# A vision layer on one core: one signal of TensorE for both halves of a product, and a new order of the work

## The chip, the cores and the metric

The kernel runs on one core of a Trainium2 chip. The metric is the device time of one execution in microseconds, lower is better. TensorE multiplies, VectorE and ScalarE work on its results, GpSimd issues gathers and computes small powers, SyncE loads and stores. Each engine executes its own list of instructions in order, and semaphores tie the lists together.

## The reference, cut to what matters

64 images of 3 x 224 x 224 are cut into 196 patches of 768 numbers each. Everything is float32.

```
h = patches @ W.T + b                                   # 768 -> 256
x = layernorm(h); xn = x / rms(x) * g
u, v, base = silu(xn @ uv_w.T)                          # 512 + 512 + 128
q, k = rope(base * gamma + beta)
kern = relu((q @ k.T + w_rel) / sqrt(128)) ** 2         # 196 x 196 per image
h = h + x * res_scale + (u * (kern @ v)) @ o_w.T
x = layernorm(h); logits = x @ W_in.T + b_in            # 8 trees of 255 nodes
walk each tree from its root by the signs of the logits (8 nodes visited)
h = h + (silu(logits) at the visited nodes, 0 elsewhere) @ W_out.T
```

## The kernel before, in words

Two images make a unit of T = 392 columns; there are 32 units. The hidden state is kept transposed, as two halves (m = 0, 1) of 128 features by 392 columns. A float32 product is made of three matmuls (`product`, lines 1144 to 1146): each operand is split into a high and a low part, ScalarE makes the high part (`high`, line 530), VectorE the low part (`low`, line 837).

The work is a software pipeline. In one pass of the loop, unit n is embedded and normalized (front), unit i goes through attention and starts its trees, and unit p = i - 1 finishes its trees. The passes at both ends, where p, i or n do not exist, are written out. The order of the calls in the four `body` functions (GpSimd, ScalarE, VectorE, TensorE) is written out, and it is the order in which each engine executes. Units are shifted between the lists: a pass of ScalarE and VectorE begins at about the middle of TensorE's.

What the change and the steps of the prediction touch:

- PSUM is full. `out_acc` sums the trees' outputs (2 banks), `hid_ps` holds two trees' logits and visits, or the embedding (4 banks), and `front` (2 banks) is used in turn by turned h, turned xn, the normalized rows turned back, base, v, u, scores, the mix, the o projection and the trees' input.
- `turn_h` turns h so that rows are tokens, for the statistics (`norm_stats`, `norm_moments` on VectorE, the power -1/2 in `norm_roots` on GpSimd, `norm_apply` and `make_xn` on ScalarE). `turn_xn` turns the result back (line 1186, eight transposes, four for each half); `xn_high` and `xn_low` split it. `turn_normed` overwrites each half of `front` with the layer norm turned back, and so waits for `xn_low` of that half; `residual` (line 901) adds it to h, and `make_base` waits for the first `residual`.
- Each of the 8 trees goes through `tree_logits`, `decisions` (line 982, the signs), `tree_visits` (line 1339, one bf16 matmul that counts how far each node is on the path), `silu_tree` (line 685), `mask` (lines 993 and 998), `hid_high`, `hid_low` and `tree_out`. Two buffers alternate, so `hid_high(i, t)` waits until `tree_out` of two trees before is whole.
- In the first four trees only the upper half of the nodes is computed; the leaf's rows are gathered: `find_leaf` (line 1368) and `leaf_number` (line 703) make the row numbers, `fetch_rows` on GpSimd (line 476) issues four indirect DMAs a tree, `leaf_dots` (line 1017), `leaf_silu` and `scale_rows` (line 720) weigh the rows, and `add_rows` (line 1380) adds them to `out_acc`.
- `project_o` makes the o projection, `update_h` (line 964) adds it to h. `turn_ffn_x` turns the trees' input.
- In the first units GpSimd also splits the late weights (`late_splits`, lines 442 and 445), and `build_rows` on ScalarE fills the table of the gathers.

TensorE signals at the end of each of these pieces; in `turn_h`, `turn_back`, `project_o` and `tree_out` at the end of each half m.

Of the kernel before, what the change touches and what calls it, by code (L numbers as in the profile page):

```python
# [44 lines left out]
DC = D // P  # L45
# [70 lines left out]
def vit_tower(nc, x, cols, tok_w, uv_w, o_w, in_w, out_w, rel, rope, anc, ident_in, out):  # L116
    ctx = ExitStack()
    with ctx:
# [317 lines left out]
        def _(pool):  # L436
# [51 lines left out]
            def body(p, i, n, nx):  # L488
                late_splits(i, n, 0)
                late_splits(i, n, 1)  # L490
                fetch_rows(i, 0, 0)
                fetch_rows(i, 0, 2)
                fetch_rows(i, 0, 1)
                fetch_rows(i, 0, 3)
                late_splits(i, n, 2)
                fetch_rows(i, 1, 0, n)
                fetch_rows(i, 1, 2)
                fetch_rows(i, 1, 1)
                fetch_rows(i, 1, 3)
                late_splits(i, n, 3)  # L500
                fetch_rows(i, 2, 0)
                fetch_rows(i, 2, 1)
                fetch_rows(i, 2, 2)
                fetch_rows(i, 2, 3)
                late_splits(i, n, 4)
# [22 lines left out]
        def _(act):  # L528
# [203 lines left out]
            def body(p, i, n, nx):  # L732
# [5 lines left out]
                if first(n):  # L738
                    build_rows()
                silu_tree(p, 7, 0)  # L740
                scale_rows(p, 3)
                silu_tree(i, 0, 0)
                hid_high(p, 7)
                norm_apply(n, 0, 0)
# [5 lines left out]
                make_xn(n, 1)  # L750
                silu_tree(i, 2, 0)
                norm_apply(n, 0, 2)
                norm_apply(n, 0, 3)
                make_xn(n, 2)
                make_xn(n, 3)
                hid_high(i, 1)
                x_high(nx, 0)
                xn_high(n, 0)
                silu_tree(i, 3, 0)
                leaf_number(i, 1)  # L760
                xn_high(n, 1)
                leaf_number(i, 2)
                x_high(nx, 1)
                hid_high(i, 2)
                silu_base(n)
                silu_v(n, 0)
                scale_base(n, 1)
                leaf_silu(i, 0)
                scale_rows(i, 0)
                silu_v(n, 1)  # L770
                v_high(n, 0)
                v_high(n, 1)
                scale_base(n, 0)
                silu_tree(i, 4, 1)
                hid_high(i, 3)
                silu_v(n, 2)
                v_high(n, 2)
                silu_v(n, 3)
                qk_high(n, 0)
                qk_high(n, 1)  # L780
                silu_u(n, 0)
                leaf_number(i, 3)
                v_high(n, 3)
                silu_tree(i, 4, 0)
                silu_tree(i, 5, 1)
                silu_u(n, 1)
# [5 lines left out]
                x_high(nx, 2)  # L792
                hid_high(i, 4)
                silu_u(n, 3)
                silu_tree(i, 5, 0)
                mix_high(n, 0)
                mix_high(n, 1)
                hid_high(i, 5)
                mix_high(n, 2)
                silu_tree(i, 6, 1)  # L800
                mix_high(n, 3)
                silu_tree(i, 6, 0)
                keep_h(i)
                leaf_silu(i, 2)
                x_high(nx, 3)
                scale_rows(i, 2)
                x_high(nx, 4)
                hid_high(i, 6)
                leaf_silu(i, 3)
                x_high(nx, 5)  # L810
# [3 lines left out]
                norm_apply(n, 1, 3)  # L814

# [19 lines left out]
        def _(dve):  # L835
# [216 lines left out]
            def body(p, i, n, nx):  # L1052
                norm_stats(n, 0, 0)
                norm_stats(n, 0, 1)
                norm_moments(n, 0)
                decisions(i, 0)
                decisions(i, 1)
                mask(i, 0)
                hid_low(p, 7)
                decisions(i, 2)  # L1060
                mask(i, 1)
                if first(n):
                    build_toward()
                hid_low(i, 0)
                decisions(i, 3)
                mask(i, 2)
                final(p)
                hid_low(i, 1)
                xn_low(n, 0)
# [4 lines left out]
                leaf_dots(i, 0)  # L1074
                rotate_qk(n, 1)
                decisions(i, 4)
                mask(i, 3)
                v_low(n, 0)
                decisions(i, 5)
                v_low(n, 1)  # L1080
                rotate_qk(n, 0)
# [3 lines left out]
                hid_low(i, 3)  # L1085
                leaf_dots(i, 1)
                mask(i, 4)
                v_low(n, 3)
                add_rel_bias(n, 0)
                add_rel_bias(n, 1)  # L1090
# [4 lines left out]
                x_low(nx, 0)  # L1095
                hid_low(i, 4)
                mask(i, 5)
                gate(n, 0)
                mix_low(n, 0)
                gate(n, 1)  # L1100
                decisions(i, 6)
# [4 lines left out]
                hid_low(i, 5)  # L1106
                mix_low(n, 3)
                x_low(nx, 1)
                leaf_dots(i, 2)
                x_low(nx, 2)  # L1110
                mask(i, 6)
                update_h(n, 0)
                update_h(n, 1)
                norm_stats(n, 1, 0)
                norm_stats(n, 1, 1)
                norm_moments(n, 1)
                x_low(nx, 3)
                leaf_dots(i, 3)
                x_low(nx, 4)
                decisions(i, 7)  # L1120
# [20 lines left out]
        def _(pe):  # L1141
# [25 lines left out]
            def turn_h(n, which, m):  # L1167
# [13 lines left out]
                last.then_inc(h_turned, 1)  # L1181

            def turn_back(src, m, done):
# [4 lines left out]
                last.then_inc(done, 1)  # L1188
# [96 lines left out]
            def project_o(n, m, es):  # L1285
# [12 lines left out]
                if es[-1] == EC - 1:  # L1298
# [43 lines left out]
            def tree_out(i, t, m):  # L1342
# [14 lines left out]
                last.then_inc(tree_added, 1)  # L1357
# [38 lines left out]
            def body(p, i, n, nx):  # L1396
                make_u(i, 0)
                tree_visits(p, 4)
                make_u(i, 1)
                tree_logits(p, 5, 1)  # L1400
                tree_out(p, 3, 0)
                tree_logits(p, 6, 0)
                scores(i, 0)
                scores(i, 1)
                tree_logits(p, 6, 1)
                add_rows(p, 1)
                tree_visits(p, 5)
                make_u(i, 2)
                make_u(i, 3)
                tree_out(p, 3, 1)  # L1410
                mix(i, 0)
                mix(i, 1)
                tree_out(p, 4, 0)
                mix(i, 2)
                mix(i, 3)
                tree_out(p, 4, 1)
                tree_visits(p, 6)
                project_o(i, 0, range(0, 3))
                project_o(i, 0, range(3, EC))
                project_o(i, 1, range(0, EC))  # L1420
                tree_logits(p, 7, 0)
                embed(n, 0)
                turn_h(i, 1, 0)
                turn_h(i, 1, 1)
                embed(n, 1)
                tree_logits(p, 7, 1)
                embed(n, 2)
                tree_out(p, 5, 0)
                embed(n, 3)
                embed(n, 4)  # L1430
                embed(n, 5)
                turn_ffn_x(i, 0)
                turn_ffn_x(i, 1)
                tree_out(p, 5, 1)
                tree_visits(p, 7)
                add_rows(p, 2)
                turn_h(n, 0, 0)
                turn_h(n, 0, 1)
                tree_out(p, 6, 0)
                tree_logits(i, 0, 0)  # L1440
                tree_logits(i, 1, 0)
                if first(n):
                    turn_rows()
                tree_visits(i, 0)
                tree_out(p, 6, 1)
                tree_logits(i, 2, 0)
                add_rows(p, 3)
                find_leaf(i, 0)
                tree_visits(i, 1)
                tree_out(p, 7, 0)  # L1450
                tree_visits(i, 2)
                tree_logits(i, 3, 0)
                find_leaf(i, 1)
                tree_out(p, 7, 1)
                tree_logits(i, 4, 0)
# [7 lines left out]
                tree_out(i, 1, 1)  # L1463
                tree_visits(i, 3)
                turn_normed(n, 1)
# [3 lines left out]
                tree_out(i, 2, 0)  # L1469
                make_v(n, 1)  # L1470
                make_v(n, 2)
                tree_logits(i, 5, 0)
                make_v(n, 3)
                tree_out(i, 2, 1)
                add_rows(i, 0)
                find_leaf(i, 3)
# [92 lines left out]
```

## Time and profile before

| | us |
|---|---|
| median of 3 runs | 2083.43 |
| lowest, highest | 2078.61, 2083.67 |
| profiled execution | 2077.75 |
| its span | 2075.9 |
| TensorE busy | 2034.1 (98%) |
| VectorE busy | 1626.5 (78%) |
| ScalarE busy | 1403.7 (68%) |
| GpSimd busy | 728.1 (35%) |

The span is the time from the first to the last instruction of the profiled execution. Busy time is a union of the rows of an engine, and matmuls overlap in their rows, since each is shown with the time that it takes through the array. In the rows PE is TensorE, DVE VectorE, ACT ScalarE, POOL GpSimd and SP SyncE.

### The profile page before, as it was taken

What the parts mean: (1) busy time and instruction counts of PE and PEld (TensorE: products, weight loads), DVE (VectorE), ACT (ScalarE), POOL (GpSimd) and SP (SyncE); (2) the same over time, 40 slices, a digit from 0 to 9 for tenths busy, and PEclk for the clock granted to TensorE, in tenths of its full rate; (3) what the DMA queues carried; (4) which work ended last, traced back from release to release, by engine and by line L of the source; (5) the groups of instructions that cost most, each with busy time, mean ns of one, the idle gap of its engine ahead of it and who ended that gap; (6) DMA issues with size and microseconds to landing.
All of it is one profiled execution on the core that took longest, in us unless ns stands there. A gap on an engine that the chain in (4) does not pass through costs nothing. (4 is left out here: it accounts for less than half of the span.)

```text
span 2075.9 us, 42491 instructions
## 1 busy us (share of the span) xinstructions
PE 2034.1 (98%) x13256; PEld 1918.2 (92%) x13256; DVE 1626.5 (78%) x4210; ACT 1403.7 (68%) x3085; POOL 728.1 (35%) x905
## 2 busy tenths in 40 slices
PE   6899999999999999999999999999999999999997
PEld 5799999999999999999999999999999999999997
DVE  5678878787877888777878787878778887778785
ACT  5556677667676667776666776676766667666665
POOL 3553343233332333333323432333323333333333
PEclk8999999999999999999999999999999999999999
DMA  5222232223222223222222322232222232222222
GB/s 159 82 80 80 82 85 67 69 70 92 81 75 68 77 70 86 80 74 70 73 81 81 85 66 70 70 93 80 74 70 77 70 85 81 74 68 72 73 71 78
DMA packets 81999, 163.13 MB, mean 79 GB/s; under 512 B 17102, under 2 KB 48048, under 8 KB 81968
## 3 DMA queue, kind: packets, MB, share of 16 engines
q0 software_dynamic: 40960, 103.02, 18.7%
q1 hardware_dynamic: 41008, 59.71, 9.7%
q8 instruction: 17, 0.28, 0.1%
q14 instruction: 14, 0.11, 0.0%
HBM read 148.76 MB, written 13.90 MB: 78 GB/s over the span
## 5 line engine op out<-in xcount | busy, mean ns | idle before, releaser
L476 POOL DMA_INDIRECT leaf_rows<-leaf_table,leaf_at x512 | 528.8, 1033 | 186.2 <-issue 186.2
L453 POOL TENSOR_TENSOR inv_root<-to_root,minus_half 98x8 f32<-98x8 f32 x64 | 94.8, 1481 | 748.7 <-DVE to_root L877 428.2
L1144 PE MATMUL out_acc<-hid_hi,outw_lo 128*128 128x392 f32 x768 | 285.4, 372 | 0.3 <-issue 0.2
L1144 PE MATMUL hid_ps<-ffn_x,in_lo 128*128 128x392 f32 x768 | 268.1, 349 | 7.9 <-POOL in_lo L445 6.9
L1145 PE MATMUL hid_ps<-ffn_x,in_hi 128*128 128x392 f32 x768 | 262.3, 342 | 0.0
L1146 PE MATMUL out_acc<-hid_hi,outw_hi 128*128 128x392 f32 x768 | 262.3, 341 | 0.0
L1145 PE MATMUL out_acc<-hid_lo,outw_hi 128*128 128x392 f32 x768 | 261.8, 341 | 0.0
L1146 PE MATMUL hid_ps<-ffn_x,in_hi 128*128 128x392 f32 x768 | 260.8, 340 | 0.0
L685 ACT ACTIVATE hid<-hid_ps,col 128x392 f32<-128x392 f32 x256 | 150.8, 589 | 124.0 <-DVE decide L982 89.0
L837 DVE TENSOR_TENSOR hid_lo<-hid,hid_hi 128x392 fp32r<-128x392 f32 (+1 forms) x256 | 197.4, 771 | 39.5 <-ACT hid_hi L530 38.8
L720 ACT ACTIVATE leaf_rows<-leaf_rows,leaf_act 98x256 f32<-98x256 f32 x512 | 218.7, 505 | 2.2
L998 DVE SCALAR_TENSOR_TENSOR hid<-hid_ps,hid 128x392 f32<-128x392 f32 x384 | 202.6, 554 | 3.4 <-remote 2.4
L1017 DVE CUSTOM_DVE_ANT_0 leaf_rows<-leaf_rows,leaf_x 98x257 f32<-98x257 f32 x512 | 188.2, 422 | 2.9 <-DMA leaf_rows<-leaf_table,leaf_at 2.9
L530 ACT ACTIVATE hid_hi<-hid 128x392 fp32r<-128x392 f32 (+1 forms) x256 | 176.0, 687 | 5.9 <-DVE hid L998 3.0
L530 ACT ACTIVATE x_hi<-x_raw 128x392 fp32r<-128x392 f32 x192 | 100.7, 525 | 111.8 <-PE hid_ps L1146 110.5
L982 DVE TENSOR_SCALAR decide<-hid_ps,col 128x392 bf16<-128x392 f32 x256 | 158.7, 620 | 21.1 <-PE hid_ps L1146 16.6
L475 POOL TENSOR_TENSOR held<-minus_half 98x1 f32<-98x1 f32 x128 | 33.0, 258 | 386.8 <-ACT v_full L616 185.5
L1144 PEld LDWEIGHTS hid_ps<-ffn_x,in_lo 128*128 128x128 f32 x768 | 144.9, 189 | 14.1 <-POOL in_lo L445 7.8
L1144 PEld LDWEIGHTS out_acc<-hid_hi,outw_lo 128*128 128x128 f32 x768 | 146.0, 190 | 2.9 <-issue 0.5
L1145 PEld LDWEIGHTS hid_ps<-ffn_x,in_hi 128*128 128x128 f32 x768 | 144.8, 188 | 2.8
L1145 PEld LDWEIGHTS out_acc<-hid_lo,outw_hi 128*128 128x128 f32 x768 | 145.7, 190 | 1.5
L530 ACT ACTIVATE xn<-u 128x392 fp32r<-128x392 f32 x128 | 68.2, 533 | 115.1 <-DVE u L949 111.2
(140 smaller groups left out, 5840.6 us busy)
## 6 DMA issues: line engine op xcount, KB each, us to landing
x_raw<-x SPq DMA_DIRECT2D x192, 196.0 KB, 2.4
out<-out_stage SPq DMA_DIRECT2D x32, 392.0 KB
leaf_rows<-leaf_table,leaf_at POOLq DMA_INDIRECT x512
leaf_table<-leaf_rows SPq DMA_DIRECT2D x4, 256.5 KB, 5.3
out_stage<-in_w SPq DMA_DIRECT2D x4, 256.0 KB
tok_major<-tok_w SPq DMA_DIRECT2D x3, 256.0 KB, 4.8
late_raw<-out_w SPq DMA_DIRECT2D x6, 128.0 KB
u<-uv_w SPq DMA_DIRECT2D x1, 576.0 KB, 3.8
```

The source lines that it names most:

```text
L453: pool.tensor_tensor(inv_root[:, 0:size], to_root[:, 0:size], minus_half[:, 0:size], ALU.pow).then_inc(roots_ok, 1)
L476: pool.indirect_dma_start(row_slot(s, g), None, table, bass.IndirectOffsetOnAxis(ap=leaf_at[:, s, g:g + 1], axis=0), element_offset=s * P ...
L530: act.activation(out, src, ACT.Copy).then_inc(done, 1)
L685: act.activation(hid_t[:, t % 2, b], hid_ps[:, t % 2, b, 0:T], ACT.Silu, bias=bias).then_inc(activated, 1)
L720: act.activation(w, w, ACT.Copy, scale=leaf_act[:, s, g:g + 1]).then_inc(rows_scaled, 1)
L837: dve.tensor_tensor(out, src, hi.bitcast(F32), ALU.subtract).then_inc(done, 1)
L982: dve.tensor_scalar(decide[:, t % 2], hid_ps[:, t % 2, 0, 0:T], c(COL_B_IN + 2 * t), 0.0, ALU.add, ALU.is_gt).then_inc(decided, 1)
L998: dve.scalar_tensor_tensor(hid_t[:, t % 2, b], hid_ps[:, t % 2, 1, 0:T], VISITED[b], hid_t[:, t % 2, b], ALU.is_ge, ALU.mult).then_inc(mas ...
L1017: dve.tensor_tensor_reduce(w, w, normed2[:, g], 1.0, 0.0, ALU.mult, ALU.add, leaf_logit[:, s, g:g + 1]).then_inc(dotted, 1)
L1144: pe.matmul(out, w[1], x_parts[0], start=start, stop=False)
L1145: pe.matmul(out, w[0], x_parts[1], start=False, stop=False)
L1146: return pe.matmul(out, w[0], x_parts[0], start=False, stop=stop)
```

## The change

TensorE gives 64 signals a unit in place of 77. `tree_out`, `turn_h`, `project_o`, `turn_xn` and `turn_ffn_x` signal once, behind the second half, and whoever waited for a half now waits for both. `turn_normed` keeps its two signals. And the order of the calls in all four `body` functions is another.

```diff
@@ scalar
-                act.wait_ge(xn_turned, 2 * n + m + 1)
+                act.wait_ge(xn_turned, n + 1)
...
-                act.wait_ge(ffn_x_turned, 2 * n + m + 1)
+                act.wait_ge(ffn_x_turned, n + 1)
...
-                    act.wait_ge(tree_added, 2 * (TREES * i + t - 1))
+                    act.wait_ge(tree_added, TREES * i + t - 1)
@@ vector
-                dve.wait_ge(h_turned, 2 * (2 * n + which) + m + 1)
+                dve.wait_ge(h_turned, 2 * n + which + 1)
...
-                dve.wait_ge(projected, 2 * n + m + 1)
+                dve.wait_ge(projected, n + 1)
...
-                dve.wait_ge(tree_added, 2 * TREES * (i + 1))
+                dve.wait_ge(tree_added, TREES * (i + 1))
@@ tensor, turn_h
-                last.then_inc(h_turned, 1)
+                if m == DC - 1:
+                    last.then_inc(h_turned, 1)
@@ turn_back
-                last.then_inc(done, 1)
+                if m == DC - 1 or done is normed_turned:
+                    last.then_inc(done, 1)
@@ project_o
-                if es[-1] == EC - 1:
+                if m == DC - 1 and es[-1] == EC - 1:
                     last.then_inc(projected, 1)
@@ tree_out
-                last.then_inc(tree_added, 1)
+                if m == DC - 1:
+                    last.then_inc(tree_added, 1)
```

The new order of TensorE, whole (a pass; products of unit p, then i, then n as named):

```
tree_visits(p, 4); tree_logits(p, 5, 1); make_u(i, 0..1); tree_out(p, 3, 0); scores(i, 0..1)
tree_logits(p, 6, 0); make_u(i, 2..3); tree_visits(p, 5); tree_logits(p, 6, 1); mix(i, 0..3)
add_rows(p, 1); tree_out(p, 3, 1); tree_visits(p, 6); project_o(i, 0, 0..2); tree_logits(p, 7, 0)
project_o(i, 0, 3); project_o(i, 1, all); embed(n, 0); tree_out(p, 4, 0); turn_h(i, 1, 0..1)
embed(n, 1); tree_out(p, 4, 1); embed(n, 2..4); tree_logits(p, 7, 1); embed(n, 5)
turn_ffn_x(i, 0..1); tree_out(p, 5, 0..1); tree_visits(p, 7); turn_h(n, 0, 0..1)
tree_logits(i, 0, 0); tree_logits(i, 1, 0); tree_out(p, 6, 0); tree_visits(i, 0)
tree_logits(i, 2, 0); add_rows(p, 2); tree_out(p, 6, 1); find_leaf(i, 0); tree_visits(i, 1)
add_rows(p, 3); tree_out(p, 7, 0); tree_visits(i, 2); tree_out(p, 7, 1); find_leaf(i, 1)
tree_logits(i, 3, 0); tree_logits(i, 4, 0); turn_xn(n, 0..1); find_leaf(i, 2)
tree_out(i, 0, 0..1); tree_out(i, 1, 0); turn_normed(n, 0); tree_out(i, 1, 1); turn_normed(n, 1)
tree_visits(i, 3); make_base(n); make_v(n, 0); tree_logits(i, 4, 1); tree_out(i, 2, 0..1)
make_v(n, 1..2); find_leaf(i, 3); make_v(n, 3); tree_logits(i, 5, 0); add_rows(i, 0)
```

Around the first turns of the trees the orders before and after read:

```diff
@@ tensor
                 tree_logits(i, 1, 0)
+                tree_out(p, 6, 0)
                 tree_visits(i, 0)
-                tree_out(p, 6, 1)
                 tree_logits(i, 2, 0)
-                add_rows(p, 3)
+                add_rows(p, 2)
+                tree_out(p, 6, 1)
@@ vector
-                norm_moments(n, 0)
                 decisions(i, 0)
+                norm_moments(n, 0)
+                mask(i, 0)
                 decisions(i, 1)
...
                 leaf_dots(i, 0)
+                mask(i, 3)
+                x_low(nx, 0)
+                x_low(nx, 1)
                 rotate_qk(n, 1)
@@ scalar
                 silu_tree(i, 0, 0)
+                hid_high(i, 0)
                 silu_tree(i, 1, 0)
                 leaf_number(i, 0)
+                norm_apply(n, 0, 0)
...
-                make_xn(n, 0)
-                hid_high(i, 0)
...
                 scale_base(n, 1)
+                v_high(n, 0)
+                scale_base(n, 0)
+                hid_high(i, 3)
+                silu_v(n, 1)
...
                 mix_high(n, 0)
+                if first(n):
+                    build_rows()
@@ gpsimd
                 fetch_rows(i, 0, 0)
+                late_splits(i, n, 2)
                 fetch_rows(i, 0, 2)
                 fetch_rows(i, 0, 1)
                 fetch_rows(i, 0, 3)
-                late_splits(i, n, 2)
```

## Rows read from the trace of the kernel before

**Rows 1.** The page, part 1: busy time, share of the span, instructions.

```profile
PE 2034.1 (98%) x13256; PEld 1918.2 (92%) x13256; DVE 1626.5 (78%) x4210; ACT 1403.7 (68%) x3085; POOL 728.1 (35%) x905
```

**Rows 2.** Stretches of the span: busy us (instructions) per engine, clock, DMA share, GB/s.

```profile
170.00:1930.00 1760.00, 1759.19 (x11557) 1664.22 (x11556) 1405.31 (x3660) 1213.37 (x2679) 592.19 (x697) 1.00 0.28 76
...
2010.00:2076.00 66.00, 54.92 (x344) 51.13 (x342) 42.19 (x113) 33.25 (x73) 19.07 (x23) 0.96 0.24 68
```

**Rows 3.** Timeline of TensorE: start us, us, line, operation; the same visit, two units.

```profile
989.19 0.34 PE L1339 MATMUL hid_ps<-decide,toward 128*128 128x392 bf16 x1
...
1052.19 0.34 PE L1339 MATMUL hid_ps<-decide,toward 128*128 128x392 bf16 x1
```

**Rows 4.** Timeline of TensorE, around visits(i, 0).

```profile
1027.73 0.34 PE L1146 MATMUL hid_ps<-ffn_x,in_hi 128*128 128x392 f32 x1
1028.06 0.34 PE L1339 MATMUL hid_ps<-decide,toward 128*128 128x392 bf16 x1
```

**Rows 5.** Timeline of VectorE, the end of norm_moments and decisions(i, 0).

```profile
1027.17 0.17 DVE L887 TENSOR_SCALAR to_root<-variance 98x4 f32<-98x4 f32 x1
1027.37 1.36 DVE L982 TENSOR_SCALAR decide<-hid_ps,col 128x392 bf16<-128x392 f32 x2
```

**Rows 6.** Timeline of TensorE, turn_xn to make_base.

```profile
1036.11 0.84 PE L1186 MATMUL front<-ident,tok_major 98*128 98x98 f32 x8
...
1038.64 0.50 PE L1186 MATMUL front<-ident,tok_major 98*128 98x98 f32 x4
...
1039.18 0.34 PE L1145 MATMUL out_acc<-hid_lo,outw_hi 128*128 128x392 f32 x1
...
1039.72 0.54 PE L1186 MATMUL front<-ident,tok_major 98*128 98x98 f32 x4
...
1040.52 0.34 PE L1145 MATMUL front<-xn,uv_hi 128*128 128x392 f32 x1
```

**Rows 7.** Timeline of ScalarE, both xn_high; in brackets idle time and releaser.

```profile
1037.05 0.50 ACT L530 ACTIVATE xn<-front 128x392 fp32r<-128x392 f32 x1 [0.31 <-PE front L1186]
...
1038.55 0.50 ACT L530 ACTIVATE xn<-front 128x392 fp32r<-128x392 f32 x1 [0.46 <-remote]
```

**Rows 8.** Timeline of VectorE, both xn_low and the residual.

```profile
1037.58 0.57 DVE L837 TENSOR_TENSOR xn<-front,xn 128x392 fp32r<-128x392 f32 x1 [0.66 <-issue]
1039.08 0.57 DVE L837 TENSOR_TENSOR xn<-front,xn 128x392 fp32r<-128x392 f32 x1 [0.93 <-ACT xn L530]
1039.56 1.36 DVE L901 SCALAR_TENSOR_TENSOR hT<-front,col,hT 128x392 f32<-128x392 f32 x2
```

**Rows 9.** Timeline of GpSimd, a gather of tree 0 beside turn_xn.

```profile
1036.62 1.15 POOL L476 DMA_INDIRECT leaf_rows<-leaf_table,leaf_at  x1 [0.30 <-issue]
```

**Rows 10.** Timeline of TensorE, the end of project_o's first half (signal at 1008.43).

```profile
1008.25 0.34 PE L1145 MATMUL front<-qk,o_hi 128*128 128x392 f32 x1
1008.43 0.34 PE L1146 MATMUL front<-xn,o_hi 128*128 128x392 f32 x1
1008.61 0.34 PE L1144 MATMUL front<-xn,o_lo 128*128 128x392 f32 x1
```

**Rows 11.** Timeline of VectorE, one dot of leaf_dots(i, 2), both update_h.

```profile
1008.03 0.42 DVE L1017 CUSTOM_DVE_ANT_0 leaf_rows<-leaf_rows,leaf_x 98x257 f32<-98x257 f32 x1
...
1010.84 1.03 DVE L964 TENSOR_TENSOR h_kept<-front,hT 128x392 f32<-128x392 f32 x2
```

**Rows 12.** Timeline of TensorE, turn_ffn_x and the product behind it.

```profile
1021.21 0.84 PE L1186 MATMUL front<-ident,leaf_x 98*128 98x98 f32 x8
...
1022.09 0.34 PE L1145 MATMUL out_acc<-hid_lo,outw_hi 128*128 128x392 f32 x1
```

**Rows 13.** Timeline of GpSimd, tree 5's late weights.

```profile
87.29 2.63 POOL L442 CAST in_hi<-out_stage 128x256 fp32r<-128x256 f32 x9
```

**Rows 14.** Waits of TensorE, first 170 us: us in total, times, longest.

```profile
PE hid_ps L1144 <- POOL in_lo L445: 6.9, 3, 4.9
```

More of the change, by code:

```diff
@@ L737, in body @@
                 copy_h(n, 1)
-                if first(n):
-                    build_rows()
                 silu_tree(p, 7, 0)
                 scale_rows(p, 3)
+                hid_high(p, 7)
                 silu_tree(i, 0, 0)
-                hid_high(p, 7)
-                norm_apply(n, 0, 0)
+                hid_high(i, 0)
                 silu_tree(i, 1, 0)
                 leaf_number(i, 0)
+                norm_apply(n, 0, 0)
                 norm_apply(n, 0, 1)
-                make_xn(n, 0)
-                hid_high(i, 0)
-                make_xn(n, 1)
-                silu_tree(i, 2, 0)
                 norm_apply(n, 0, 2)
                 norm_apply(n, 0, 3)
+                silu_tree(i, 2, 0)
+                make_xn(n, 0)
+                make_xn(n, 1)
                 make_xn(n, 2)
@@ L756, in body @@
                 hid_high(i, 1)
+                xn_high(n, 0)
+                xn_high(n, 1)
                 x_high(nx, 0)
-                xn_high(n, 0)
+                leaf_number(i, 1)
+                hid_high(i, 2)
+                x_high(nx, 1)
+                leaf_number(i, 2)
                 silu_tree(i, 3, 0)
[L760 to L764, printed above, removed]
                 silu_base(n)
                 silu_v(n, 0)
+                leaf_silu(i, 0)
                 scale_base(n, 1)
-                leaf_silu(i, 0)
+                v_high(n, 0)
+                scale_base(n, 0)
+                hid_high(i, 3)
+                silu_v(n, 1)
                 scale_rows(i, 0)
-                silu_v(n, 1)
-                v_high(n, 0)
                 v_high(n, 1)
-                scale_base(n, 0)
+                silu_v(n, 2)
                 silu_tree(i, 4, 1)
-                hid_high(i, 3)
-                silu_v(n, 2)
+                leaf_number(i, 3)
                 v_high(n, 2)
+                silu_tree(i, 4, 0)
+                qk_high(n, 0)
                 silu_v(n, 3)
-                qk_high(n, 0)
                 qk_high(n, 1)
                 silu_u(n, 0)
-                leaf_number(i, 3)
                 v_high(n, 3)
-                silu_tree(i, 4, 0)
+                silu_u(n, 1)
+                x_high(nx, 2)
                 silu_tree(i, 5, 1)
-                silu_u(n, 1)
                 leaf_silu(i, 1)
@@ L791, in body @@
                 silu_u(n, 2)
-                x_high(nx, 2)
+                silu_u(n, 3)
                 hid_high(i, 4)
-                silu_u(n, 3)
+                mix_high(n, 0)
+                if first(n):
+                    build_rows()
                 silu_tree(i, 5, 0)
-                mix_high(n, 0)
                 mix_high(n, 1)
-                hid_high(i, 5)
+                silu_tree(i, 6, 1)
                 mix_high(n, 2)
-                silu_tree(i, 6, 1)
                 mix_high(n, 3)
                 silu_tree(i, 6, 0)
+                hid_high(i, 5)
                 keep_h(i)
+                x_high(nx, 3)
+                x_high(nx, 4)
                 leaf_silu(i, 2)
-                x_high(nx, 3)
                 scale_rows(i, 2)
-                x_high(nx, 4)
+                x_high(nx, 5)
                 hid_high(i, 6)
-                leaf_silu(i, 3)
-                x_high(nx, 5)
                 norm_apply(n, 1, 0)
@@ L1068, in body @@
                 hid_low(i, 1)
+                decisions(i, 3)
                 xn_low(n, 0)
@@ L1074, in body @@
                 leaf_dots(i, 0)
+                mask(i, 3)
+                x_low(nx, 0)
+                x_low(nx, 1)
                 rotate_qk(n, 1)
+                hid_low(i, 3)
                 decisions(i, 4)
-                mask(i, 3)
                 v_low(n, 0)
-                decisions(i, 5)
+                rotate_qk(n, 0)
                 v_low(n, 1)
-                rotate_qk(n, 0)
+                leaf_dots(i, 1)
                 v_low(n, 2)
@@ L1089, in body @@
                 add_rel_bias(n, 0)
+                decisions(i, 5)
                 add_rel_bias(n, 1)
@@ L1094, in body @@
                 kern_low(n, 1)
-                x_low(nx, 0)
+                decisions(i, 6)
+                gate(n, 0)
                 hid_low(i, 4)
-                mask(i, 5)
-                gate(n, 0)
+                gate(n, 1)
                 mix_low(n, 0)
-                gate(n, 1)
-                decisions(i, 6)
                 gate(n, 2)
@@ L1105, in body @@
                 gate(n, 3)
-                hid_low(i, 5)
+                mask(i, 5)
                 mix_low(n, 3)
-                x_low(nx, 1)
-                leaf_dots(i, 2)
                 x_low(nx, 2)
                 mask(i, 6)
+                hid_low(i, 5)
+                decisions(i, 7)
                 update_h(n, 0)
                 update_h(n, 1)
+                leaf_dots(i, 2)
+                x_low(nx, 3)
                 norm_stats(n, 1, 0)
@@ L1116, in body @@
                 norm_moments(n, 1)
-                x_low(nx, 3)
+                x_low(nx, 4)
                 leaf_dots(i, 3)
-                x_low(nx, 4)
-                decisions(i, 7)
                 x_low(nx, 5)
@@ L1425, in body @@
                 embed(n, 1)
[L1426 removed]
+                tree_out(p, 4, 1)
                 embed(n, 2)
[L1428 removed]
                 embed(n, 3)
                 embed(n, 4)
+                tree_logits(p, 7, 1)
                 embed(n, 5)
@@ L1463, in body @@
                 tree_out(i, 1, 1)
+                turn_normed(n, 1)
                 tree_visits(i, 3)
-                turn_normed(n, 1)
                 make_base(n)
@@ L1469, in body @@
                 tree_out(i, 2, 0)
+                tree_out(i, 2, 1)
                 make_v(n, 1)
                 make_v(n, 2)
+                find_leaf(i, 3)
+                make_v(n, 3)
                 tree_logits(i, 5, 0)
-                make_v(n, 3)
-                tree_out(i, 2, 1)
                 add_rows(i, 0)
-                find_leaf(i, 3)
             body(None, None, None, 0)
```

58 lines of the change are left out of this document (27 added, 31 removed).

## The prediction

> **What bounds the kernel now.** I read the page's busy shares first: TensorE is busy 98% of the span, VectorE 78%, ScalarE 68% [rows 1]. The table of stretches then shows that TensorE is busy in 1759.19 of the 1760 us between 170 and 1930 us, at full granted clock (the 2.4 GHz level), and that what it idles lies at the two ends [rows 2]. So time can be won in the middle only if TensorE has fewer or denser starts. A matmul's row is 0.34 us long while the next one starts 0.18 us later, so a wait shorter than about 0.16 us, and part of any longer one, is hidden inside "busy"; the place to look is the distance between starts. One unit (two images, 414 matmuls) lasts 1052.19 - 989.19 = 63.00 us, from the same instruction of one unit to that of the next [rows 3].
>
> Two places of each unit have a hole between starts.
>
> - Visits of tree 0: its matmul starts 1028.06 - 1027.73 = 0.33 us after the one before it, where 0.18 is usual: 0.15 us lost [rows 4]. It waits for decisions(i, 0), whose row on VectorE begins at 1027.37 right behind the eleven small rows of norm_moments [rows 5].
> - From the second turn_normed to make_base: 1040.52 - 1039.72 = 0.80 us for four transposes and one product matmul, where the first turn_normed has 1039.18 - 1038.64 = 0.54: 0.26 us lost [rows 6]. Behind it is a late signal. All eight transposes of turn_xn end at 1036.11 + 0.84 = 1036.95. ScalarE starts xn_high(0) at 1037.05, but xn_high(1) at 1038.55, after 0.46 us of idling with nothing of its own in the way [rows 7]. So the second half's signal, 1.6 us late, pushes xn_low(1) to 1039.08 and both residual rows to 1039.56 to 1040.92 [rows 8]. In that stretch the gather rows of GpSimd are issued and land [rows 9].
>
> **What the change does to the sum, part by part.** Numbers are per unit, and the profiled execution (2077.75 us, span 2075.9, so 1.85 around it) is what they are taken from; it stands 5.7 us below the median of 2083.43.
>
> 1. Thirteen signals fewer: 8 of tree_out, 2 of turn_h, 1 each of turn_xn, turn_ffn_x and project_o. The last matmul of project_o's first half, at 1008.43, carries one and the next starts 0.18 us later; the distance before it, without a signal, is 0.18 too (1008.25 to 1008.43) [rows 10]. So on TensorE I take a signal as free; with rounding it is worth at most 0.01 us, 13 x 0.01 x 32 = 4 us for all. Below zero it can't be.
>    On the waiting side, the first half's consumer now waits for the second half too. norm_stats(n, 0, 0) waits 0.44 us more, and the first update_h one half product of 12 x 0.178 = 2.1 us. Both still fit: in the new order turn_h(i, 1) starts 2.1 us after the o projection ends, and both update_h take 1.03 us [rows 11]. xn_high(0) loses nothing: it started at 1037.05, after both halves were done anyway [rows 7].
>    The Trainium skill ("TensorE: Matmul & The Clock Gate", The cost: per-tile semaphore tail) says that increments serialize and gives 26.3 ns for each. By that alone the change would save 13 x 32 x 26.3 ns = 11 us; [rows 10] show no such gap between starts.
>
> 2. The new order of TensorE. I laid it out with the distances between starts that the rows have: 0.178 for a product matmul, 0.84 for eight transposes with their end [rows 6], and so on, with time 0 at visits(p, 4). Places: scores 3.9, visits 5 8.2, mix 9.5 to 14.8, project_o 16.2 to 21.6, turn_h(i, 1) 23.7, turn_ffn_x 32.0, turn_h(n, 0) 35.1, logits 0 35.9, visits 0 39.2, turn_xn 47.9, turn_normed 50.4 and 51.3, make_base 51.9, end 62.6.
>    - Hole 1 closes: one product of tree_out(p, 6) now stands between logits 1 and visits 0, and decisions(i, 0) stands ahead of norm_moments. norm_stats needs until 37.6, so decisions end near 38.2, 0.9 us before visits 0. Gain 0.15.
>    - Hole 2 closes if the signal of turn_xn comes in time: it is complete at 48.8, xn_high and xn_low of half 0 take 0.50 + 0.57 us with 0.1 of handing over [rows 7, 8], so turn_normed(0) could go at 50.0 and is due at 50.4; half 1 and the residuals (0.5 us a piece in a row) end near 52.4, and make_base needs only the first, at 51.6. Gain 0.26.
>    - Small groups among the products cost at their end. Eight turn_ffn_x transposes to the second product matmul take 1022.09 - 1021.21 = 0.88 us, against 8 x 0.084 + 0.178 = 0.85: 0.03 per group [rows 12]. There are 16 such groups where there were 14, but add_rows(p, 3) and visits 1 stay joined and the four mix are no longer cut in two. Net loss about 0.02, between -0.05 and +0.10.
>    - New close calls: hid_high(i, 0) on ScalarE needs tree_out(p, 6) to be whole, 42.3 in the new order, while it is reached near 38.8. ScalarE stands for 3.5 us there, and behind it stand silu of tree 1, leaf_number(0), the four norm_apply and make_xn. They take some 5 us and end at 47.4, 0.5 before turn_xn. silu_v(1), behind scale_base and hid_high(3), ends at 59.2 for make_v(3) at 59.5. I give 0.05 for these; if one of them slips, each 0.1 us is 3 us of the total.
>
> 3. VectorE, ScalarE and GpSimd. Their issue changes only in order; x_low(nx, 0) and (nx, 1) move to 55 us, 3 us and more behind their x_high, and SyncE can load the next chunks sooner. add_rows(p, 1) moves behind the mix, so the last four gathers of a unit start 7.5 us later; their dots have over 3 us left by my layout. Cost 0; uncovered it would be one leaf_dots, 4 x 0.42 = 1.7 us [rows 11].
>
> 4. The ends of the program. GpSimd splits the late weights there; tree 5's now stand ahead of three of the first four gathers. In the old order that split began at 87.29 [rows 13] and TensorE waited 6.9 us in three places for such weights [rows 14]; now the first dots come up to 8 us later and the weights up to 4 earlier. build_rows moves behind the first mix_high (+1 us). I take 0, between -4 and +5.
>
> Sum: (0.15 + 0.26 - 0.02 - 0.05) = 0.34 us a unit. Of 32 units some 30 run in the steady pattern: 10.2 us. 2077.75 - 10.2 = 2067.6 for such an execution, and 2083.43 - 10.2 = 2073 for the median.
>
> **Rivals.**
>
> - *A, the merged signal comes late (slower).* In [rows 7] one signal of turn_xn got through at once and the other took until 1038.55, 2.44 us after turn_xn's start. The new single signal is completed at the same phase as the second was, while the gathers run just as before. If it fares like that one, xn_high(0) starts at 47.9 + 2.44 = 50.35, xn_low(0) ends at 51.5, and turn_normed(0), due at 50.4, slips by 1.1 us. 30 x (1.1 - 0.34) = +23 us: 2106. It bites from a delay of 0.4 us on (50.0 against 50.4); from 0.75 on the whole is slower. For it: a signal late by 1.6 us at this very place. Against: the first of two passed, and now there is only one in the queue.
> - *B, no change.* The holes close but others of the same size open: TensorE's signal of project_o may fall among the later gathers and be held, ScalarE has less room behind hid_high(i, 0), the start loses a few us. 0.3 to 0.4 us a unit, net nothing: 2083.
> - *C, signals cost TensorE time.* Then 4 us by the bound of part 1 come on top: 2069. (By the page's figure above it would be 11 us and 2062.) Against it stand [rows 10].
> - *D, the signals are not fewer in effect*: the waits ask for n + 1 where they asked for 2n + 2, the same event. Then only the order counts and the sum stands; it has no time of its own.
>
> **Numbers.** Forecast with C: 0.54. A in full or in part: 0.27. B: 0.19. A measurement of this kernel tells about 0.3% (6.2 us) from no change. Faster 0.56, same 0.17, slower 0.27. The forecast's own range is 2064 to 2079; with 8 in 10 wanted it has to take in most of A: 2064 to 2104.
>
> **What would show it.** Right: the unit's period falls from 63.0 to 62.6 or 62.7; no distance over 0.2 us ahead of visits 0; make_base's first two rows 0.29 us or less behind the transposes; xn_high(0) within 0.2 us of the end of turn_xn. A: ScalarE idle ahead of xn_high(0) for over 1 us, and a hole ahead of the first turn_normed. B: period near 63, holes ahead of turn_h(i, 1), turn_xn or make_v(3). The forecast is wrong if the period grows, or if the ends of the program move by over 5 us.

## The result and the profile after

The changed kernel takes 2103.59 us (median of 4 runs, 2101.80 to 2106.85) where the kernel before takes 2083.34: ratio 1.0104, 95% interval 1.0085 to 1.0124. It is 20 us slower. The forecast said 10 us faster; rival A, with a chance of 0.27, had 2106. The profiled execution took 2102.87 us, 25.1 more than that of before.

The page's first part, beside [rows 1]: GpSimd is 88 us busier, TensorE 3 us, the other two are less busy. Most of GpSimd's part is the issue of its gathers, 1157 ns on average where it was 1033; the other profiles of the new order have 1149 to 1161, x2 aside (1033).

```profile
PE 2037.1 (97%) x13256; PEld 1920.4 (91%) x13256; DVE 1610.3 (77%) x4210; ACT 1392.5 (66%) x3085; POOL 815.8 (39%) x905
```

The table of stretches, beside [rows 2] (us, then busy us and instructions of PE, PEld, DVE, ACT, POOL, then clock, DMA share, GB/s):

```profile
170.00:1930.00 1760.00, 1744.82 (x11469) 1650.42 (x11468) 1383.19 (x3628) 1197.88 (x2660) 670.41 (x691) 1.00 0.28 76
...
2010.00:2101.00 91.00, 78.42 (x485) 73.19 (x483) 59.41 (x152) 50.05 (x111) 34.92 (x37) 0.94 0.26 72
```

TensorE now idles 15.2 us in the middle, where it idled 0.8. The timeline of TensorE shows one such place (start us, us, line, operation, in brackets idle time and releaser); it answers to [rows 6]. The first row is turn_xn, the row at 1113.42 the same transposition one unit later.

```profile
1049.63 0.84 PE L1187 MATMUL front<-ident,tok_major 98*128 98x98 f32 x8
...
1051.96 0.34 PE L1146 MATMUL out_acc<-hid_hi,outw_hi 128*128 128x392 f32 x1
1053.14 0.56 PE L1187 MATMUL front<-ident,tok_major 98*128 98x98 f32 x4 [0.83 <-DVE xn L837]
...
1113.42 0.84 PE L1187 MATMUL front<-ident,tok_major 98*128 98x98 f32 x8
```

From 1051.96 to the first turn_normed there are 1.18 us, where 0.18 is usual. The unit takes 63.79 us, where [rows 3] had 63.00. ScalarE beside it, which answers to [rows 7], and VectorE, which answers to [rows 8], in two fences:

```profile
1051.99 0.89 ACT L530 ACTIVATE xn<-front 128x392 fp32r<-128x392 f32 x2 [2.48 <-remote]
```

```profile
1052.52 1.04 DVE L837 TENSOR_TENSOR xn<-front,xn 128x392 fp32r<-128x392 f32 x2 [1.88 <-ACT xn L530]
```

The eight transposes of turn_xn start at 1049.63 and end 0.84 later, at 1050.47. ScalarE had idled since 1049.51, and xn_high(0) starts at 1051.99: the signal is 1.5 us late. Over the 28 units of the loop the distance ahead of turn_normed(0) is 1.18 to 1.21 us in 17, 0.48 to 0.53 in 10 and 0.18 in one; the mean is 0.91.

I cut both executions at two like places, the end of turn_xn in the first and in the last unit of the steady pattern (27 units apart):

| us | to the first turn_xn | 27 units | from the last on | span |
|---|---|---|---|---|
| before | 217.2 | 1702.7 | 156.1 | 2075.9 |
| after | 225.2 | 1715.5 | 160.4 | 2101.0 |
| difference | +8.0 | +12.8 | +4.3 | +25.1 |

So half of the loss is in the steady units, half at the ends.

### The profile page after: what moved, and what is told of

Read it like the earlier page. It is cut to its first block and busy times, and to the rows that moved or that the text cites. A ratio compares the mean times of both kernels' runs of the same rounds, so it can differ in the third digit from the quotient of the medians.

```text
span 2101.0 us, 42239 instructions
## 1 busy us (share of the span) xinstructions
PE 2037.1 (97%) x13256; PEld 1920.4 (91%) x13256; DVE 1610.3 (77%) x4210; ACT 1392.5 (66%) x3085; POOL 815.8 (39%) x905
## 5 line engine op out<-in xcount | busy, mean ns | idle before, releaser
L476 POOL DMA_INDIRECT leaf_rows<-leaf_table,leaf_at x512 | 592.1, 1157 | 181.9 <-issue 181.7
L1144 PE MATMUL hid_ps<-ffn_x,in_lo 128*128 128x392 f32 x768 | 283.4, 369 | 1.7 <-POOL in_lo L445 1.5
```

Source lines behind the costliest of these rows:

```text
L476: pool.indirect_dma_start(row_slot(s, g), None, table, bass.IndirectOffsetOnAxis(ap=leaf_at[:, s, g:g + 1], axis=0), element_offset=s * P ...
L1144: pe.matmul(out, w[1], x_parts[0], start=start, stop=False)
```

## The experiments

Five sets of kernels ran, each on one chip with the kernel before timed beside it (profiled on A, C and D only). A signal is called held, or late, when it is posted well after the last instruction of its piece has ended; posted at once, it comes 14 ns behind it. The period is the mean of the 27 units, and a "hole" a distance between starts that is longer than usual. B, C, D, E are the chips of these sets in order (the fifth set was on C again), A that of the result (whether it is one of the others isn't known). The first four kernels ran on B.

**One signal pair back, and all of them.** Edit of the first, in the changed kernel (the second undoes all five merges alike):

```diff
-                act.wait_ge(xn_turned, n + 1)
+                act.wait_ge(xn_turned, 2 * n + m + 1)
@@ turn_back
-                if m == DC - 1 or done is normed_turned:
+                if m == DC - 1 or done is not ffn_x_turned:
```

> The changed kernel, with one of its five merges undone: turn_xn signals each half again (65 signals a unit). Theory H (a signal of TensorE that completes while the gathers' traffic runs is held back): of two signals one gets through by about 49.0 on the unit's clock, as before; xn_high(0) starts then, turn_normed(0) has no hole, make_base keeps one of up to 0.3 us. Period 62.8 to 63.1 us in place of 63.8, time 2072 to 2085. Rival R (what is late is the end of turn_xn in the new order, by whatever signal): period stays at 63.5 to 63.9, time 2097 to 2104.

Measured 2084.79 against 2074.10 for before (ratio 1.0051, 1.0034 to 1.0067), period 62.88 (the kernel before on A: 63.06). The timeline of ScalarE:

```profile
1038.45 0.50 ACT L530 ACTIVATE xn<-front 128x392 fp32r<-128x392 f32 x1 [0.65 <-PE front L1187]
1040.24 0.50 ACT L530 ACTIVATE xn<-front 128x392 fp32r<-128x392 f32 x1 [1.29 <-PE front L1187]
```

The first half's signal is on time, the second half's is 1.5 us late here (all eight end at 1038.76; in other units 0.7), and the hole ahead of turn_normed(0) is gone. R falls.

> The changed kernel with all five merges undone: new order alone, 77 signals a unit. H: like x1, period 62.8 to 63.1, time 2072 to 2085; the order alone then gives what the forecast said of it or a part. Rival O (the order costs the time): 2097 to 2104. Against x1 it has 12 signals a unit more: rival C (26 ns of TensorE each) puts it 10 us above x1, free signals put it within 2 us of x1.

2080.51 (1.0028, 1.0018 to 1.0038), period 62.85. The order alone doesn't cost the 20 us. It has twelve signals a unit more than the kernel with turn_xn's pair alone (x1 above) and isn't slower than it. In most units its first signal of turn_xn is held as well, by 0.2 to 0.3 us, without making TensorE late.

**The merges alone**: the changed waits and signals of the diff, all five, with the calls of the kernel before in their old order.

> The kernel before in its old order, with the five merges alone (64 signals a unit). H: turn_xn ends at the same phase of the gathers as before, 48.92, and its one signal is held to 49.7 or 50.5; turn_normed(0), due at 50.0, slips 0.5 to 1.3 us in nearly every unit: period 63.5 to 64.2, time 2095 to 2115. Rival O (the new order costs the time, the signals are harmless): 2079 to 2084, no change. Rival C (a signal costs TensorE 26 ns): 2072.

2103.66 (1.0141, 1.0124 to 1.0159), 29.6 us over before: H holds, O and C fall. The hole has two parts. Timeline of TensorE at visits 0, then ScalarE at xn_high(0):

```profile
1041.39 0.34 PE L1341 MATMUL hid_ps<-decide,toward 128*128 128x392 bf16 x1 [0.42 <-DVE decide L982]
```

```profile
1051.06 0.50 ACT L530 ACTIVATE xn<-front 128x392 fp32r<-128x392 f32 x1 [0.98 <-PE front L1187]
```

The distance ahead of visits 0 is 0.76 us (0.33 in [rows 4]), since norm_stats(n, 0, 0) waits for both halves of turn_h; the merged turn_xn signal is 0.78 us late and makes 0.25 more.

**No gather in flight at turn_xn.** GpSimd holds the four gathers of tree 0 of the changed kernel:

```diff
+                    if s == 0:
+                        pool.wait_ge(xn_hi_ok, 2 * n + 2)
```

> The changed kernel, its 64 signals kept, but the four gathers of tree 0 wait on GpSimd until both xn_high of the unit are done, so that none is in flight when turn_xn ends. Theory H: the merged signal posts at once, xn_high(0) starts within 0.1 us of the end of turn_xn, no hole ahead of turn_normed(0), period 62.7 to 62.8, time 2066 to 2074 unless the later gathers (3 us later) make leaf_dots or add_rows(i, 0) late. Rival R (merging alone delays the signal, whatever GpSimd does): hole of 0.5 to 1.2 us stays, 2100 or more.

Both things happened. (H said that the signal would be on time, and that the later gathers could cost something.) Here the merged signal posts 14 ns behind the end of turn_xn in every unit, though the other profiles of this chip have a signal of turn_xn held. ScalarE shows it (turn_xn starts at 1037.57 and ends 0.84 later), and TensorE shows the price:

```profile
1038.44 0.89 ACT L533 ACTIVATE xn<-front 128x392 fp32r<-128x392 f32 x2 [1.00 <-PE front L1190]
```

```profile
1052.33 0.47 PE L1147 MATMUL front<-uv_hi,xn 128*98 128x512 f32 x1 [2.85 <-ACT v_full L619]
```

Signals beside the moved gathers are held now: in this unit one of make_v completes at 1049.04 and is posted at 1050.46, and find_leaf's completes at 1049.48 and is posted at 1051.97.

The time is 2214.54 (1.0674, 1.0654 to 1.0695). The gathers end 6 us later, and on ScalarE leaf_silu(i, 0), which waits for them, stands ahead of silu_v(1), which make_v(3) waits for. I had named leaf_dots as late, not this queue, and had priced it at nothing. Where TensorE idled 2.85 us, the clock fell as well in 19 of 27 units, in four of them before the hole was over: products then start 0.327 us apart, not 0.178. In the other 8 units the same hole left it at 1.00. Two stretches, one ahead of the hole above, one around a hole at which it fell:

```profile
1000.00:1050.00 50.00, 49.38 (x328) 46.66 (x327) 36.14 (x100) 29.03 (x64) 16.40 (x20) 1.00 0.23 64
...
1252.00:1256.00 4.00, 2.67 (x6) 1.88 (x7) 3.70 (x7) 4.00 (x10) 0.00 (x0) 0.51 0.56 161
```

**Only the fourth gather held** (chip C):

```diff
+                if g == 3 and n is not None:
+                    pool.wait_ge(xn_hi_ok, 2 * n + 2)
+                    pool.tensor_tensor(gate[:, :], minus_half[:, 0:1], minus_half[:, 0:1], ALU.mult).then_inc(gate_ok, 1)
```

> The changed kernel (64 signals), with only the fourth gather of tree 0 held until both xn_high are done (by one small row on GpSimd that waits for it, 0.2 us). Theory I (TensorE's signals are held only once GpSimd has issued the fourth of four gathers back to back; in six traces all signals that completed 0.2 to 0.8 us behind that issue were held): xn_high(0) starts within 0.1 us of the end of turn_xn, period 62.7 to 62.8 us, 2066 to 2074 where the kernel before takes 2074. Theory F (the traffic in flight holds them: gathers two and three are still in flight at 48.9): the signal stays 0.8 to 1.5 us late, period 63.5 and more, 2090 or more.

> The kernel before (77 signals, old order) with the same hold of the fourth gather. Theory I: the second signal of turn_xn, 1.6 us late before, is on time; the hole of 0.2 to 0.3 us ahead of make_base goes, period 62.75 to 62.85, 5 to 9 us faster than before. Theory F: no change, within 2 us of before.

> The kernel before, unchanged, for a profile on the same chip as the others: period 63.04, start and tail of TensorE's idling as before (30 and 7 us) if the chip makes no difference; if the ends differ between chips, here they differ from the first profile by the 9 us by which its median was lower on the second chip.

The third of these decided the set: on chip C the kernel before, with its gathers as ever, has no signal held anywhere. Its period is 62.75 and not 63.06, and its median 2070.43 and not 2083.34. So the two edits had nothing to cure, and I and F are not told apart: x5 has 2081.84 (1.0062, 1.0046 to 1.0079) and x6 2073.62 (1.0017, 1.0008 to 1.0027), 3 us slower than before. Theory I as a plain rule doesn't fit the traces of A and B themselves. In the five with the gathers as ever (x2 left out), 169 of 176 recorded signals that completed 0.9 to 1.0 us behind the start of a tree's fourth issue were posted within 30 ns, while 291 of 312 that completed 1.1 to 1.7 us behind one were not.

**The start as before**, in the kernel with the fourth gather held (late_splits(i, n, 4) goes back as well, behind the gathers of tree 2, and build_rows on ScalarE behind copy_h(n, 1)):

```diff
                 fetch_rows(i, 0, 0)
-                late_splits(i, n, 2)
                 fetch_rows(i, 0, 2)
                 fetch_rows(i, 0, 1)
                 fetch_rows(i, 0, 3, n)
+                late_splits(i, n, 2)
```

> x5_fourth_gather_held with the start of the program as before (GpSimd's late splits behind the first four gathers, build_rows behind the second copy of h). If the new places of these cost the 4 us by which the first steady unit is later in the new order with 77 signals, this is 3 to 5 us faster than x5; if not they cost nothing, it is within 1 us of x5 or slower.

2079.01 (1.0044, 1.0027 to 1.0060); its first steady turn_xn ends 3.7 us earlier than in x5. The new places of the late splits and build_rows cost that.

**The changed kernel where nothing is held** (chip D):

> The changed kernel again, beside a profile of the kernel before on the same chip, because in the last four profiles (among them the kernel before) no signal of TensorE was held at all, while in the six before every one had held signals. Theory H2 (the hold comes with the chip or the loading, and the merge turns it into a loss): where the profile of before shows the second turn_xn signal held, this has the hole ahead of turn_normed(0), a period of 63.5 to 63.9 and about 20 us more than before; where before shows none held, this has period 62.7 to 62.8 and is slower than before by its ends alone, 5 to 12 us. Rival (the merge always costs): about 20 us more whatever the profile of before shows.

> The changed kernel with the fourth gather held, beside the changed kernel on the same chip. On a chip with holds: theory I (the fourth back-to-back gather does it): signal on time, period 62.75, 18 to 22 us faster than the changed kernel; theory F (traffic in flight does it): same as the changed kernel. On a chip without holds both say within 2 us of it.

> New order, 77 signals. On a chip without holds it has what the changed kernel has; if signals cost TensorE time (26 ns each, 13 a unit) it is 11 us slower than the changed kernel there, if they are free within 2 us. On a chip with holds: 18 to 25 us faster than the changed kernel.

> The kernel before, for its profile: period 63.04 and the second turn_xn signal 1.6 us late if this chip holds signals, 62.75 and both on time if not.

D holds none either. The changed kernel takes 2082.70 against 2071.00 (1.0054, 1.0038 to 1.0071), as H2 said. ScalarE of the changed kernel, whose turn_xn runs from 1041.15 to 1041.99, with GpSimd's fourth gather beside it as ever (two fences):

```profile
1042.02 0.89 ACT L530 ACTIVATE xn<-front 128x392 fp32r<-128x392 f32 x2 [1.00 <-PE front L1187]
```

```profile
1041.69 0.97 POOL L476 DMA_INDIRECT leaf_rows<-leaf_table,leaf_at  x1 [0.30 <-issue]
```

Here turn_xn ends 0.30 us behind the start of the fourth issue (1041.99 - 1041.69), just as on A (1050.47 - 1050.17), and the signal is posted at once.

The kernel before on D (y4) shows what its ScalarE does where nothing is held. turn_xn runs from 1032.58 to 1033.42:

```profile
1033.12 0.50 ACT L530 ACTIVATE xn<-front 128x392 fp32r<-128x392 f32 x1
```

xn_high(0) starts 0.30 us before turn_xn ends. In [rows 7] it starts 0.10 us after the end, so the first of the two signals was late there too, by 0.4 us; in six units of that trace it was 1.1 us.

The fourth gather held changes nothing (2083.15), the order alone takes 2078.98 (1.0039, 1.0025 to 1.0054). The same table for chips D and E:

| us | to the first turn_xn | 27 units | from the last on |
|---|---|---|---|
| before (D) | 217.7 | 1694.2 | 154.8 |
| order alone (D) | 221.5 | 1695.1 | 159.1 |
| changed kernel (D) | 226.0 | 1694.7 | 160.5 |
| merges alone (E) | 222.8 | 1707.5 | 156.1 |
| changed kernel (E) | 225.7 | 1694.3 | 159.3 |

> Old order, 64 signals. Holding chip: again about 30 us above before. Chip without holds: xn_high(0) on time; what stays is the later norm_stats(n, 0, 0), 0.43 us a unit ahead of visits 0 (13 us), and the start 5 to 6 us later than before: 16 to 20 us above before. If merging cost nothing but through held signals it would be within 3 us of before there.

E holds none. z4, the merges alone, takes 2087.83 (1.0094, 1.0077 to 1.0111): merging costs 0.43 us a unit ahead of visits 0 and 5 us at the start even so. The changed kernel in the same set:

> The changed kernel on this chip. Holding chip: period 63.5 to 63.9, 25 to 30 us above before. Chip without holds: 62.77, 11 to 12 us above before, all of it in the ends (8 us until the first steady unit, 5 us in the tail).

> The changed kernel with the fourth gather held, beside the changed kernel, a third time, to meet a chip that holds signals. Holding chip: theory I (the fourth issue back to back does it) signal on time, period 62.75, 18 to 22 us faster than the changed kernel; theory F (traffic in flight) no better than it. Chip without holds: within 2 us of it.

2081.73 and 2082.23 (both 1.0064, 1.0047 to 1.0080).

**The forecast's own gain alone**, in the kernel before (E):

```diff
-                norm_moments(n, 0)
                 decisions(i, 0)
+                norm_moments(n, 0)
```

> The kernel before with two calls of VectorE swapped: decisions(i, 0) ahead of norm_moments(n, 0). It closes the hole ahead of visits 0 (0.15 us a unit): period 62.60 on a chip without holds, 62.90 with, 4 to 5 us faster than before, if norm_moments, 0.6 us later, makes nothing late. Rival: its powers and norm_apply come 0.6 us later and turn_xn waits; then a hole of the same size opens there and the time is that of before.

2095.41 (1.0130, 1.0113 to 1.0147), 26.6 us slower: the rival came true and worse. The hole ahead of visits 0 is gone, but norm_moments ends later, and what follows from it comes too late on ScalarE, whose make_xn ends just before:

```profile
1043.61 0.91 ACT L579 ACTIVATE tok_major<-tok_major,xn_scale 98x256 f32<-98x256 f32 x2
```

```profile
1044.57 0.89 PE L1186 MATMUL front<-ident,tok_major 98*128 98x98 f32 x8 [0.34 <-ACT tok_major L579]
```

The distance ahead of turn_xn is 0.67 us, and there are two smaller ones ahead of tree_out(p, 7, 0) and visits 2; the period is 63.55.

**The last set** (C again) met no held signals and repeated the start:

> The changed kernel with the fourth gather held and GpSimd's late splits and build_rows in their old places, beside the changed kernel. On a chip that holds signals: theory I gives signals on time and a period of 62.77 against 63.5 to 63.8, together with the start 22 to 26 us faster than the changed kernel; theory F gives the same late signal in both and 3 to 4 us. On a chip that holds none: period as in the changed kernel, the first steady unit 3.7 us earlier, 3 to 4 us faster in all.

> The changed kernel on this chip: 2101 to 2107 with a period of 63.5 to 63.9 if the chip holds signals, 2080 to 2084 with 62.77 if not.

2078.15 (1.0036, 1.0024 to 1.0049) and 2083.17 (1.0064, 1.0047 to 1.0080), the first steady turn_xn 3.1 us earlier. Theories I and F stay open.

No kernel that ran beats the kernel before.

## Why the prediction was wrong

1. *Signals are free on TensorE*: right. Order alone and changed kernel on D differ by 13 signals a unit and by 0.01 us in the period (62.78, 62.77). The Trainium skill ("TensorE: Matmul & The Clock Gate", The cost: per-tile semaphore tail) gives 26.3 ns for each increment behind a set of small packed tiles; carried over to these large matmuls, as an estimate, it would be 13 x 26.3 ns = 0.34 us a unit, and the traces have under a tenth of that.
2. *The waiting side, "both still fit"*: right in the new order for turn_h and the o projection (no hole there). In the old order the merges make the distance ahead of visits 0 0.43 us longer in every unit (norm_stats waits for both halves of turn_h); the new order has none of that. "xn_high(0) loses nothing" was wrong: its start in [rows 7], behind the end of both halves, was itself due to a late signal.
3. *Hole 1 closes, +0.15*: right, 0.18 us ahead of visits 0 after. But a hole that I had not named opened ahead of the scores, where the qk operand is late. Timeline of TensorE, the last product before and the first two matmuls of the scores:

```profile
1005.22 0.34 PE L1146 MATMUL out_acc<-hid_hi,outw_hi 128*128 128x392 f32 x1
1005.48 0.33 PE L1144 MATMUL front<-qk 128*98 128x196 f32 x1
1005.64 0.25 PE L1145 MATMUL front<-qk 128*98 128x196 f32 x1
```

   0.26 and 0.16 us stand here, where before had 0.18 and 0.09: 0.12 to 0.15 lost again.
4. *Hole 2 closes "if the signal of turn_xn comes in time"*: this is the step that failed in the steady units. On A the signal came 1.5 us late in 17 of 28 units and 0.8 in 10, as [rows 7] had shown for one of two. I set against it that "the first of two passed, and now there is only one in the queue". That misread the rows: the first had been late too, by 0.4 us, as the kernel before on D shows (y4). In x1 it is posted on time, 0.3 us before the other completes and is held. The merge does away with just that early signal. The single late one then stops xn_high(0), with no half of the work ahead of it.
   Rival A was right in place and kind. Its price was 1.1 - 0.34 = 0.76 us a unit; measured was 63.54 - 63.06 = 0.48 in the mean. The slip was 1.0 us in 17 units, but 0.32 in 10, which is 0.77 in the mean against the same kernel on D (63.54 - 62.77). The gain under it is 0.29 if D's period is what A would have without late signals (63.06 - 62.77), near the 0.34. But it is all hole 2: on D the new order and the merges together gain nothing (62.77 against 62.75), since there hole 2 isn't there to close, and what hole 1 gives back is lost at other places (step 3).
5. *The ends at 0, between -4 and +5*: this step failed too, and by as much: +8.0 and +4.3 on A, +8.3 and +5.7 on D. These 12.3 us alone are more than the 10.2 us that the forecast had to win, and on C, D and E, where no signal is late, the changed kernel is 12 to 13 us slower by them. The order costs 4 at the start, of which 3 to 4 are the late splits and build_rows (x7; w1, which also holds a gather). Merging costs another 4 to 5 there (4.5 on D; 5.1 between E and D), and it points to turn_xn's merge: x1 and the order alone both reach the first steady turn_xn at 221.4 to 221.5 on B, the changed kernel at 225.1 to 226.0 on A, C, D and E (it didn't run on B). In the fill the first turn_normed waits 1.19 us in place of 0.53, and TensorE is granted less in the stretch behind it; that the lower clock makes the rest of the 4 to 5 us is argued, not shown. The stretch 30 to 40 us on D of the order alone, then of the changed kernel, TensorE's clock third from the end:

```profile
30.00:40.00 10.00, 8.89 (x36) 6.54 (x36) 6.94 (x12) 7.95 (x16) 1.92 (x3) 0.91 0.01 2
```

```profile
30.00:40.00 10.00, 8.58 (x33) 6.34 (x31) 4.93 (x9) 7.01 (x13) 2.80 (x5) 0.73 0.01 2
```

   At the tail TensorE waits 4.6 us for the trees' last input ([rows 2] has the stretch; before it was 3.2). The waits of TensorE from 1950 us on, changed kernel:

```profile
PE front L1187 <- ACT leaf_x L569: 4.6, 1, 4.6
PE hid_ps L1341 <- ACT hid L685: 1.3, 1, 1.3
PE hid_ps L1371 <- issue: 1.3, 1, 1.3
```

   In part 4 I had weighed the late weights alone. Those did get better: TensorE's waits for them ([rows 14]) fell from 6.9 to 1.5 us, and new ones of the same size took their place. The waits of TensorE in the first 170 us, changed kernel:

```profile
PE front L1144 <- ACT v_full L616: 4.2, 3, 2.6
PE hid_ps L1371 <- DVE taken L993: 3.7, 1, 3.7
PE hid_ps L1144 <- DVE x_lo L837: 2.6, 2, 1.3
...
PE hid_ps L1144 <- POOL in_lo L445: 1.5, 1, 1.5
```

Open: what holds the signals. Shown is that the holds follow the gathers (x2 on B: the signal of turn_xn is on time without them, and signals beside the moved gathers are held), and that a signal of turn_xn is held in nearly all units of five profiles on A and B (before, changed, x1, x3, x4). On C, D and E it is held in none of eight profiles with the gathers as ever (x8, y1, y3, y4, z1, z3, z4, w2), nor in the six with the fourth gather held by the edit, and the same kernel has it on one chip and not on another. Whether the chip, or how the program was loaded, decides is not shown; nor whether the fourth issue or the traffic does it, since no chip with held signals was met again. One rival more is untested: the recording itself. The six profiles of A and B hold 17196 to 18298 records of semaphore updates, the fourteen of C, D and E 22191 to 22732, so on A and B about a fifth is missing, those of VectorE and ScalarE among them. Held signals and missing records always come together here, and no run tells which brings the other.

## What to carry to other kernels

A signal on the first half of a product costs TensorE nothing that these runs can measure, and it lets the consumer start early. Merging it moves the consumer to the latest possible time, and in x1 it was the early signal that got through while the later one was held. Weigh the fill and the drain of a pipeline by themselves: here the merged wait of turn_xn went from 0.53 to 1.19 us in the fill, with no other unit's work over it, and the ends lost as much as the steady units. Before you call a signal on time, ask when its work ended, and not only whether the consumer idled. And a hole of 0.15 us that an order leaves can be the price of something behind it; close it only after following every later call on that engine.

## What the runs showed of the hardware

- TensorE's signals were posted 0.2 to 1.6 us late beside GpSimd's indirect DMAs on A and B, and 14 ns behind the end on C, D and E. Of VectorE's and ScalarE's recorded ones none was held, but some of their records are missing there. In the kernel before it goes with 0.31 us a unit (period 63.06 on A, 62.75 on C and D), an estimate of 9 us in all (30 units). On B, which held signals too, that kernel takes 2074.10 and has no profile, so what it costs there isn't known.
- At a hole of 2.85 us TensorE fell to its lower level in 19 of 27 units (granted clock 0.51 over 4 us, products 0.327 us apart) and stayed at the higher one in 8; holes of 0.83 us never did that (1.00 over 1760 us).
